# Cross-attention in a decoder layer: the softmax division moves from the attention output to the rows of the output projection, and the projections are dealt to other turns of the loop

## The reference, cut to what matters

```python
kv = jnp.concatenate([context, latents], axis=1)
q = rms_norm((latents @ Wq)...heads..., q_norm_w)
k = rms_norm((kv @ Wk)...heads..., k_norm_w)
v = (kv @ Wv)...heads...
scores = jnp.einsum('bhgqd,bhkd->bhgqk', qg, k) * scale
probs = jax.nn.softmax(scores, axis=-1)
out = jnp.einsum('bhgqk,bhkd->bhgqd', probs, v)
return out.reshape(bsz, q_len, HEADS * HEAD_DIM) @ Wo
```

## Time and profile before

| | |
|---|---|
| time, median of 3 runs | 3009.77 us (3009.34 to 3010.96) |
| profiled execution: its own time | 3008.26 us |
| profiled execution: its span, first to last instruction | 3006.5 us |
| PE busy, share of the span | 2777.4 us, 92% |
| POOL busy | 2410.9 us, 80% |
| DVE busy | 2197.1 us, 73% |
| ACT busy | 2072.1 us, 69% |
| mean granted TensorE clock | 0.956 of 2.4 GHz |

### The profile page before, as it was taken

One profiled execution on the slowest core, in us unless ns is written; L12 is line 12 of the kernel. 1 busy time (PEld: TensorE's weight loads), 2 busy tenths in 40 slices (PEclk: granted clock), 3 DMA queues, 4 the chain that ended last, 5 costly groups with the idle time before them and its releaser, 6 DMA issues. The chain is left out here.

```text
span 3006.5 us, 46930 instructions
## 1 busy us (share of the span) xinstructions
PE 2777.4 (92%) x14860; PEld 2229.0 (74%) x14860; DVE 2197.1 (73%) x3447; ACT 2072.1 (69%) x3868; POOL 2410.9 (80%) x2241
## 2 busy tenths in 40 slices
PE   2229999999999999999999999999999999999976
PEld 1128888888888888888888888888888888888744
DVE  6726777777777777777777777777777777777754
ACT  1115777777777777777777777777777777777751
POOL 4413888888888888888888888888888888888880
PEclk7659999999999999999999999999999999999995
DMA  1075343344434434344433434434433333333201
GB/s 35 28 250 191 127 139 132 129 143 129 141 124 134 146 127 141 127 134 137 142 127 130 147 129 132 137 125 137 147 111 115 127 115 110 112 114 113 71 7 67
DMA packets 155749, 370.32 MB, mean 123 GB/s; under 512 B 12778, under 2 KB 46572, under 8 KB 155505
## 3 DMA queue, kind: packets, MB, share of 16 engines
q1 hardware_dynamic: 153752, 365.49, 37.0%
q10 hardware_dynamic: 1752, 1.84, 0.2%
HBM read 329.53 MB, written 37.75 MB: 122 GB/s over the span
## 5 line engine op out<-in xcount | busy, mean ns | idle before, releaser
L1140 DVE SCALAR_TENSOR_TENSOR running_max<-S_ps,rk,running_max 128x512 f32<-128x512 f32 (+1 forms) x896 | 669.1, 747 | 254.4 <-ACT scores L954 247.5
L954 ACT ACTIVATE scores<-S_ps,rk 128x512 f32<-128x512 f32 (+1 forms) x960 | 653.8, 681 | 225.0 <-PE S_ps L759 220.6
L682 POOL TENSOR_TENSOR P_lo<-P,P_hi 128x512 fp32r<-128x512 f32 x512 | 674.7, 1318 | 129.1 <-ACT P L970 128.9
L1124 DVE TENSOR_TENSOR scores<-scores,Mb_ps 128x512 f32<-128x512 f32 (+1 forms) x960 | 648.2, 676 | 166.3 <-PE Mb_ps L876 166.3
L700 POOL TENSOR_TENSOR acc<-acc,scores 128x512 f32<-128x512 f32 (+1 forms) x448 | 586.8, 1310 | 120.0 <-ACT scores L970 77.1
L757 PE MATMUL S_ps<-QT_hi,KT_hi 128*128 128x512 f32 (+1 forms) x960 | 559.0, 582 | 2.1 <-DVE running_max L1140 1.2
L700 POOL TENSOR_TENSOR acc<-acc,P 128x512 f32<-128x512 f32 x384 | 524.8, 1367 | 0.0
L757 PE MATMUL K_ps<-Wkv_hi,kvT 128*128 128x256 f32 (+1 forms) x1664 | 469.8, 282 | 1.7 <-DVE V_full L1180 1.0
L759 PE MATMUL K_ps<-Wkv_hi,kvT 128*128 128x256 f32 (+1 forms) x1664 | 470.5, 283 | 0.0
L758 PE MATMUL K_ps<-Wkv_lo,kvT 128*128 128x256 f32 (+1 forms) x1664 | 469.7, 282 | 0.0
L787 PE MATMUL OT_ps<-scores,V_full 128*128 128x512 f32 (+1 forms) x896 | 459.9, 595 | 0.0
(11 more groups left out here) (189 smaller groups left out, 5442.3 us busy)
## 6 DMA issues: line engine op xcount, KB each, us to landing
kvT<-kvT_scratch SPq DMA_DIRECT2D x416, 512.0 KB, 3.3
w_stage<-in_L_xattn_Wq SPq DMA_DIRECT2D x64, 512.0 KB, 4.4
w_stage<-in_L_xattn_Wo SPq DMA_DIRECT2D x64, 512.0 KB, 4.3
kvT_scratch<-built SPq DMA_DIRECT2D x60, 512.0 KB, 2.9
xrow<-in_ctx SPq DMA_DIRECT2D x48, 256.0 KB
w_stage<-in_L_xattn_Wk SPq DMA_DIRECT2D x32, 256.0 KB, 2.9
w_stage<-in_L_xattn_Wv SPq DMA_DIRECT2D x32, 256.0 KB, 3.2
xT<-kvT_scratch SPq DMA_DIRECT2D x8, 512.0 KB, 5.3
```

The costliest lines, as they stand in the source:

```text
L682: e.tensor_tensor(P_lo[n % 2][0:r, :], P_sb[n % 2][0:r, :], f(P_hi[n % 2][0:r, :]), ALU.subtract)\
L954: e.activation(row[s % RING][0:r, :], S_ps[s % 2][0:r, :], ACT.Copy, scale=rk[0:r, v % 2, j:j + 1])\
L1124: e.tensor_tensor(d, d, Mb_ps[0:r, :], ALU.add).then_inc(s_d, 1)
L1140: e.scalar_tensor_tensor(a, src, k, a, ALU.mult, ALU.max).then_inc(s_top, 1)
```

## The change

The division by the row sums leaves the transposed attention output. Now ACT makes `OT_hi` from `OT_ps` and DVE makes `OT_lo` from `OT_ps` in the step after the last `pv` of the half; the buffer `OT_n`, its copy, the multiply by the reciprocals and the transposes `RB` are gone. The output projection runs for each head `g` and part `t` by itself (four parts of three matmuls, where there were two of six), and DVE adds each to `y` with the reciprocal of its rows as a factor. The first `pv` of the next half now waits for `OT_lo`. The running maximum has two buffers, so its first tile of a half waits for the `MT` transposes of two halves before. Nearly all jobs of the table have other places: the query projections stand at 1, 3 and, for the next unit, 25 and 27; the last of them comes six places earlier, and so does `normalise` (place 7 in place of 13). The weight splits stand at places 2, 5, 9, 14 and 21 in place of 5, 11, 15, 19 and 25.

```diff
@@ fill(s)
+            if s in (-AHEAD - 2, -AHEAD - 1):
+                jobs.append(("Q", 0, 0, s + AHEAD + 2))
...
             0: [("KT", v - 1, 3)],
-            1: [("Q", v, 0, 0)],
-            3: [("Q", v, 0, 1)],
-            5: [("X", b + 1, 2 * h), ("MT", 2 * v - 2)],
-            7: [("Q", v, 1, 0)],
-            9: [("Q", v, 1, 1)],
-            10: [("AT", 2 * v - 3)],
-            11: [("O", 2 * v - 4, 0)],
-            13: [("O", 2 * v - 4, 1)],
-            15: [("RB", 2 * v - 3), ("QT", v, 0)],
-            17: [("KT", v, 0)],
+            1: [("Q", v, 1, 0)],
+            3: [("Q", v, 1, 1)],
+            5: [("O", 2 * v - 4, 1, 0), ("O", 2 * v - 4, 1, 1)],
+            6: [("MT", 2 * v - 2)],
+            7: [("X", b + 1, 2 * h)],
+            9: [("QT", v, 0)],
+            11: [("AT", 2 * v - 3)],
+            13: [("O", 2 * v - 3, 0, 0), ("O", 2 * v - 3, 0, 1)],
+            15: [("KT", v, 0)],
+            17: [("O", 2 * v - 3, 1, 0), ("O", 2 * v - 3, 1, 1)],
             19: [("KT", v, 1)],
             20: [("MT", 2 * v - 1)],
-            21: [("O", 2 * v - 3, 0)],
-            23: [("O", 2 * v - 3, 1)],
-            25: [("AT", 2 * v - 2), ("KT", v, 2)],
-            27: [("RB", 2 * v - 2), ("QT", v, 1)],
-            29: [("X", b + 1, 2 * h + 1)],
+            21: [("QT", v, 1)],
+            23: [("X", b + 1, 2 * h + 1)],
+            25: [("Q", v + 1, 0, 0), ("AT", 2 * v - 2)],
+            26: [("KT", v, 2)],
+            27: [("Q", v + 1, 0, 1)],
+            29: [("O", 2 * v - 2, 0, 0), ("O", 2 * v - 2, 0, 1)],
@@ splits(s)
-            chunk = {5: ("Wkv", v + 1, 0), 11: ("Wq", v + 1, 0), 15: ("Wo", v - 2, 1), 19: ("Wq", v + 1, 1),
-                     25: ("Wo", v - 1, 0)}.get(c)
+            chunk = {2: ("Wkv", v + 1, 0), 5: ("Wq", v + 1, 0), 9: ("Wo", v - 2, 1), 14: ("Wq", v + 1, 1),
+                     21: ("Wo", v - 1, 0)}.get(c)
@@ SP: the query tiles of the next batch
-                if c == 22 and 0 <= v < UNITS - 1 and v % KVH == KVH - 1:
+                if c == 10 and 0 <= v < UNITS - 1 and v % KVH == KVH - 1:
@@ PE
                 if j == 0 and p:
-                    e.wait_ge(s_ot, p)
+                    e.wait_ge(s_ol, p)
...
-            def output(p, t):
+            def output(p, g, t):
                 v, half = divmod(p, 2)
-                if t == 0:
+                if g == 0 and t == 0:
                     e.wait_ge(s_ol, p + 1)
                     e.wait_ge(s_wl, W_AT["Wo", v, half] + 1)
-                out = take(("O", p, t))
-                for g in range(2):
-                    ins = three(out, OT_hi[:, g, t * P:(t + 1) * P], OT_lo[:, g, t * P:(t + 1) * P],
-                                Wo_hi[:, g, :], Wo_lo[:, g, :], g == 0, g == 1)
-                ins.then_inc(s_ff, 1)
+                out = take(("O", p, g, t))
+                three(out, OT_hi[:, g, t * P:(t + 1) * P], OT_lo[:, g, t * P:(t + 1) * P],
+                      Wo_hi[:, g, :], Wo_lo[:, g, :], True, True).then_inc(s_ff, 1)
@@ ACT, after exp(s - WAIT) of the step after the last pv
-                e.activation(OT_n[:], OT_ps[:], ACT.Copy).then_inc(s_ot, 1)
+            def OT_high(p):
+                e.wait_ge(s_pv, NJ * (p + 1))
+                if p:
+                    e.wait_ge(s_ff, F_AT["O", p - 1, 1, 1] + 1)
+                e.activation(OT_hi[:].rearrange("p g q -> p (g q)"), OT_ps[:], ACT.Copy).then_inc(s_ot, 1)
@@ DVE: raise_max
-            a = top[0:r, :]
+            a = top[p % 2][0:r, :]
...
-                    if p:
-                        e.wait_ge(s_ff, F_AT["MT", p - 1] + 1)
+                    if p >= 2:
+                        e.wait_ge(s_ff, F_AT["MT", p - 2] + 1)
@@ DVE: drain
-                elif job[0] == "RB":
-                    p = job[1]
-                    e.wait_ge(s_ot, p + 1)
-                    e.tensor_tensor(OT_n[:], OT_n[:], out, ALU.mult).then_inc(s_fr, 1)
...
-                    e.tensor_tensor(y[:, t, :], y[:, t, :], out, ALU.add).then_inc(s_fr, 1)
+                    e.scalar_tensor_tensor(y[:, t, :], out, rinv[:, p % 2, 2 * g + t:2 * g + t + 1], y[:, t, :],
+                                           ALU.mult, ALU.add).then_inc(s_fr, 1)
@@ DVE: OT_low, now directly after raise_max of the same step as OT_high
-                e.wait_ge(s_oh, p + 1)
-                e.tensor_tensor(OT_lo[:].rearrange("p g q -> p (g q)"), OT_n[:],
+                e.wait_ge(s_ot, p + 1)
+                e.tensor_tensor(OT_lo[:].rearrange("p g q -> p (g q)"), OT_ps[:],
                                 f(OT_hi[:]).rearrange("p g q -> p (g q)"), ALU.subtract).then_inc(s_ol, 1)
```

More of the change, by code:

```diff
@@ L363, in real @@
                 return job[1] < B and job[2] < NJ
-            return 0 <= job[1] < (HALVES if job[0] in ("RB", "O", "MT", "AT") else UNITS)
+            return 0 <= job[1] < (HALVES if job[0] in ("O", "MT", "AT") else UNITS)
         return [x for x in jobs if real(x)]
@@ L463, in cross_attention @@
         sq = sb("sq", [P, 4, HD])
-        top = sb("running_max", [P, QW])
+        top = [sb(f"running_max{i}", [P, QW]) for i in range(2)]
         acc = [sb(f"acc{i}", [P, QW]) for i in range(2)]
-        OT_n = sb("OT_n", [P, QW])
         OT_hi = sb("OT_hi", [P, 2, S], F32R)
@@ L510, in cross_attention @@
         s_ot = sem("OT_copied")
-        s_oh = sem("OT_hi_copied")
         s_ol = sem("OT_lo_copied")
@@ L652, in _ @@
                 for x in fill(s - 2):
-                    if x[0] == "O" and x[2] == 1 and (x[1] + 1) % (2 * KVH) == 0:
+                    if x[0] == "O" and x[2:] == (1, 1) and (x[1] + 1) % (2 * KVH) == 0:
                         b = x[1] // (2 * KVH)
@@ L866, in turn_max @@
                 for i in range(4):
-                    ins = e.transpose(out[:, i * P:(i + 1) * P], top[:, i * P:(i + 1) * P], ident[:])
+                    ins = e.transpose(out[:, i * P:(i + 1) * P], top[p % 2][:, i * P:(i + 1) * P], ident[:])
                 ins.then_inc(s_ff, 1)
@@ L921, in _ @@
                         turn_sums(x[1])
-                    elif x[0] == "RB":
-                        spread_reciprocal(x[1])
                     else:
-                        output(x[1], x[2])
+                        output(*x[1:])
                 if 0 <= s - WAIT - LAG < NS:
@@ L1089, in _ @@
                 if last >= 0 and last % NJ == 0 and last // NJ < HALVES:
-                    copy_OT(last // NJ)
+                    OT_high(last // NJ)
                 for kind, v in rooted(s - 2):
@@ L1210, in drain @@
                     e.reciprocal(rinv[:, p % 2, :], sums[:, p % 2, :]).then_inc(s_ri, 1)
[L1211 to L1217 removed]
+                else:
+                    _, p, g, t = job
+                    if g == 0 and t == 0:
+                        e.wait_ge(s_ri, p + 1)
+                    if p % (2 * KVH) == 0 and g == 0 and t == 0:
                         e.wait_ge(s_yd, 32 * (p // (2 * KVH)) + 16)
[L1219 removed]
+                    if g or p % (2 * KVH):
+                        old = ("O", p, 0, t) if g else ("O", p - 1, 1, t)
+                        e.wait_ge(s_fr, F_AT[old] + 1)
+                    e.scalar_tensor_tensor(y[:, t, :], out, rinv[:, p % 2, 2 * g + t:2 * g + t + 1], y[:, t, :],
+                                           ALU.mult, ALU.add).then_inc(s_fr, 1)
             def OT_low(p):
[L1222 to L1223 removed]
+                e.wait_ge(s_ot, p + 1)
+                e.tensor_tensor(OT_lo[:].rearrange("p g q -> p (g q)"), OT_ps[:],
                                 f(OT_hi[:]).rearrange("p g q -> p (g q)"), ALU.subtract).then_inc(s_ol, 1)
@@ L1230, in _ @@
                     raise_max(s - 1)
+                last = s - WAIT - LAG - NJ
+                if last >= 0 and last % NJ == 0 and last // NJ < HALVES:
+                    OT_low(last // NJ)
                 for what in squared(s - 1):
@@ L1240, in _ @@
                         normalise(v)
-                for x in fill(s - 2):
-                    if x[0] == "RB":
-                        OT_low(x[1])
 def feed_forward(nc, y_in, Wr, rb, eb, out):
```

21 lines of the change are left out of this document (3 added, 18 removed).

## The result

The changed kernel takes 3059.52 us (median of 4, 3057.02 to 3062.22) against 3010.05 before (3009.34 to 3010.96): ratio 1.0164, 95% interval 1.0147 to 1.0182, 1.6% slower. The profiled execution took 3057.02 us with a span of 3055.2, 48.8 us more than before. The forecast was 3040.

The account below looks back on a forecast made before the run. PE, full by its matmul starts, was taken to set the pace. Terms: -27.9 (`RB`) - 12 (hole) + 78 (hold) - 8 (end) = +30 us on 3008.3, median forecast 3040 us; own range 3020 to 3060, wider range 2992 to 3066.

Parts of the forecast that it names:

- PE sets the pace by its starts: Steady loop: PE is full by matmul starts, so removing the `RB` transposes gives back 64 x 0.436 = 27.9 us.
- The hole at place 19: PE's 0.39 us wait for POOL's `P_lo` goes entirely, as weight splits leave places 15 to 19: -12 us.
- The hold at place 10: First `pv` waits for `OT_lo` until T+10.0, PE ready T+7.4 (T: `spread_max` start, place 7): 30 x 2.6 = +78 us.
- `normalise` delays `shift`: On DVE at place 7, `normalise` now stands ahead of the first `shift`, moving it from T+0.63 to T+2.35.
- rival B: `normalise` does not delay `shift`, only ACT's queue counts: hold 1.2 us at place 10, 2998 us; chance 0.12.
- `OT_lo` 0.68 and not 1.54: DVE's `OT_lo` from PSUM takes 0.68 us; 1.54 would cost 30 x 0.86 = 26 us more.
- Place 25 without a hold: Same chain without `normalise`, two more PE jobs in front: `OT_lo` ready some 0.2 us before PE, nothing added.
- The end: After the last add, the stretch to the store of `y` falls from 14.5 to about 6 us: -8 us.
- The start costs nothing: SP's tile loads wait at most for one POOL split, two steps before use at the earliest; nothing added.
- A: Rival: no hold at all, PE waits for nothing new, 2962 us; chance 0.14.
- C: Rival: removed transposes were free, PE's 28 us don't come back, 3068 us; chance 0.14 together with D's larger forms.
- D: Rival: place 25 holds 0.5 us in 31 units, or `OT_low` takes 1.54 us: 3056 to 3066; larger forms and C 0.14.

Follow-up runs that it names:

- experiment 7: version 5 with the four transposes of the running maximum issued twice in each half; 3009.3 us, ratio 0.9999 to the kernel before.
- Experiment 12: version 5 with POOL's split of `Wq` at place 15 instead of 14; 2982.5 us, ratio 0.9910 to the kernel before.
- version 5: Changed kernel with the `Wo` split moved to place 10, `normalise` to place 13 and `QT` to place 15; 2982.8 us, ratio 0.9906 to the kernel before.
- 2: Changed kernel with `normalise` back at place 13 and `QT` back at place 15; 3010.8 us, ratio 1.0003 to the kernel before.
- 3: Changed kernel with `QT` alone back at place 15, `normalise` staying at place 7; 3042.0 us, ratio 1.0110 to the kernel before.
- 1: Changed kernel with ACT's split of `Wo` moved from place 9 to place 10; 3020.3 us, ratio 1.0038 to the kernel before.
- 6: Changed kernel where ACT first copies `OT_ps` to SBUF, the first `pv` waits for that copy alone, and `OT_hi`, `OT_lo` are made from it; 3082.8 us.
- 8: Version 6 with `OT_low` on DVE one step later, behind the `raise_max` that stood behind it; 3027.8 us, ratio 1.0059 to the kernel before.
- 4: Changed kernel with the key and value projection at place 10, ahead of the held `pv`, computed twice; 3050.6 us, ratio 1.0139 to the kernel before.
- experiment 9: version 5 with every weight chunk's load issued two steps later on SP; 2976.6 us, ratio 0.9888 to the kernel before.

## Why the prediction was right, step by step

The direction, the mechanism and the range held; the likeliest time was 20 us low. At 3059.5 us the result lies only 0.5 us inside the forecast's own range of 3020 to 3060. That is partly luck: the range was made from doubt about the hold, which came out 7 us smaller than forecast, and two terms put at nothing, the clock and the start, added 20 us.

*PE sets the pace by its starts.* Right. Forecast 27.9 us for `RB`; experiment 7 puts as many transposes back and pays 26.6. The rule of the Trainium skill (Perfetto Trace Analysis, Identifying the Most-Contended Engine) that judges PE's headroom by the weight loads' share would leave PE room for them; the measurement decides for the starts here. A share of 81% was not 19% of room.

*The hole at place 19, -12 us.* The size held (PE's waits for `P_lo` fall out of the list); the reason given was one of two. I had put it down to the weight splits leaving places 15 to 19. Experiment 12 puts a split back at 15 and no hole comes: PE asks later, since places 15 to 18 take 10.98 us there, with a part of the output projection at 17, where they took 10.04. So in version 5 the moved splits are not needed. In the changed kernel itself, with `QT` still at place 9, these places take 10.56 us, and `P_lo` would end, 1.16 us later than it does (the shift between versions 5 and 12), just when PE asks for it. Whether it would be in time there was not run, and neither was a version with the splits moved and PE not later.

*The hold at place 10, 30 x 2.6 = +78.* Right in place, queue and cause. Step by step the chain was forecast 0.3 us too long from the start: `shift` T+2.35, measured T+2.05, because `normalise` takes 2.38 us for two at this place and not 2.65. From there the steps held, and the 0.3 us stayed to the end: second `exp` 4.9 against 4.61, `pv` 10.0 against 9.69. PE was ready at 7.67, forecast 7.37: the `raise_max` behind the delayed `shift` also holds up PE's scores at place 9 by 0.3 us, which I had not followed. A unit without `X` has 9.90 and 8.12; there the scores of place 9 are 0.7 us late, and the trace shows the wait, one that I had not named:

```profile
2418.47 0.50 PE L758 MATMUL S_ps<-QT_hi,KT_hi 128*128 128x512 f32 x1 [0.41 <-DVE running_max L1121]
```

Against the 7.38 that PE needs with no slip (version 5's 6.94 and the 0.44 of `QT`) the loss is 2.31 us in 19 units and 2.52 in 11: 71 us for the 78 forecast.

*`normalise` delays `shift`* (rival B denied it). Shown by 2 and 3: 31 us are its part. *The split is in the queue:* shown by 1, 28.5 us. *The wait for `OT_low` and not for a copy:* 0.7 us of the hold, shown by 6 and 8. No one of them made the hold; with either of the first two gone half of it stays (1.06 and 1.08 us), and with both 0.13 us are left.

*`OT_lo` 0.68 and not 1.54.* 0.69 measured from PSUM. By the Trainium skill (SBUF — State Buffer, Who interferes with whom) two SBUF inputs collide with a reading POOL instruction. The trace agrees: in version 6, with two, it is 1.65 us beside POOL's weight split and 0.69 beside POOL's work on four columns, in the rows above.

*Place 25 without a hold.* Right, and as near as forecast: in the unit whose `Mb_ps` starts at 1051.95, `OT_lo` ends at 1101.01 and the `pv` starts at 1101.25. All 30 new waits ahead of a `pv` are at place 10.

*The end, -8.* From the last add's end (2976.70) to the store of `y` (2984.50) it is 7.8 us and was 14.5: -6.7. From the 61st `Mb_ps` (the last of the full units) to that store it is 147.2 us and was 156.8: -9.6. This stretch also holds six query matmuls, twelve of the output projection and five `RB` fewer than before, so not all of the 9.6 is the shorter end.

*The granted clock stays.* Not forecast, +9.5 us; it is a price of the hold, as 1, 3 and 4 show, since the drops go when the idle stretch is shorter.

*The start costs nothing.* Wrong, the largest miss. The first `Mb_ps` comes 7.7 us later and the first unit takes 2.6 us more. I had written that the tile loads wait at most for one POOL split. They do, but at the start that one wait is 17 us, and experiment 9 gets about 6 us back. Most of what is left is work that has moved here: six more query matmuls ahead of the first `Mb_ps` (48 where there were 42), and in the first unit twelve matmuls of the output projection for the four transposes of one `RB`. At 0.23 us a start that is an estimated 1.4 and 2.3 us, and the same matmuls are missing at the end.

The sum, over the profiled executions, by stretches: +10.3 to the end of the first unit; +47.5 in the 29 units behind it; -9.6 from the 61st `Mb_ps` to the store of `y`; together 48.2 of the 48.8 us. The 47.5 are -25 (`RB`, 29 x 0.87), -11 (the hole), +68 (the hold in these units), +9.5 (the clock) and 6 that are left. Those lie mostly in the ten units that have no `X` at place 23, with 0.4 to 0.5 us each where the others have 0.1. There the scores of place 24 start right behind a `raise_max` of DVE, at 2458.51 behind one that ends at 2458.45, so it is a small wait of the same kind as at place 9. No run takes it away.

*The rivals.* A (no hold, 2962) is out by the 30 waits. B (2998) is out by `shift`, which starts at T+2.05 and not within 0.3 us of `Mb_ps`, and by 2 and 3. C is out by 7. D's two forms, 3056 to 3066, did not happen; that the time falls among theirs is chance.

## What to carry to other kernels

Where PE is full, a unit is a chain plus a rest: work that leaves the chain but stays on PE gives back only the difference (`QT`: 0.58 less 0.44), while work of another engine that leaves the chain gives all as long as PE still waits (the split: 0.95). Before letting a wait stand on a longer route (a copy and then a subtraction on another engine), count what is queued ahead of each of its steps on its own engine, and behind it, what the waiting instruction holds up: version 6 mended the first and lost 55 us by the second. The change as made was 1.6% slower with a schedule in which three jobs stood at the wrong places (`normalise`, `QT` and the `Wo` split), and 0.9% faster with them moved; a result of the whole says nothing yet of its parts.

## What the hardware showed that I had not expected

The granted clock fell behind a hold of 2.0 us of an otherwise full PE, 0.1 to 0.9 us after PE had gone on, for 3.4 us, and only in some of the holds: 6 of the 19 of that length in the changed kernel, none of the 11 others, with 1.7 to 1.8 us, none in the versions with shorter holds, none when 1.4 of the 2.0 us were filled with doubled matmuls. What picks the six was not found. One such drop costs 1.4 to 1.6 us, nearly as much as the hold itself. The same `normalise` pair took 2.38 us at place 7 and 2.65 at place 13, a difference not traced to a cause. `OT_lo` took 0.69 us from PSUM, and with both inputs in SBUF 1.65 beside a large POOL instruction and 0.69 beside small ones. The POOL add that overlaps the end of the long `OT_lo` took 1.74 us, where most adds of 512 columns take 1.3.
